# Attention scores as four masked full-array products, the product with v as eight of 66 columns, q scaled before the scores

## The reference

```python
q = rms_norm(layernorm(x) @ w_q.T + b_q, g_q)
k = rms_norm(ctx @ w_k_img.T + b_k_img, g_k_img)      # ctx: 64 rows
v = ctx @ w_v_img.T + b_v_img
p = softmax(q_h @ k_h.T / 4)                          # per head, 64 x 64
x = x + concat(p @ v_h) @ w_o.T + b_o
```

## Time and profile before

| | us |
|---|---|
| median of three runs (911.7 to 912.24) | 911.82 |
| span of the profiled execution | 1005.5 |
| busy in that span: PE / DVE / ACT / POOL | 846.2 / 590.8 / 471.5 / 480.1 |
| attention steps, from the first instruction to 450.7 us and their drain to about 525 | 525 |
| expert tiles, 525 to 875 | 350 |
| combine pass, to the end | 130 |

### The profile page before, as it was taken

One profiled execution on the slowest core, in us unless ns is written; L12 is line 12 of the kernel. 1 busy time (PEld: TensorE's weight loads), 2 busy tenths in 40 slices (PEclk: granted clock), 3 DMA queues, 4 the chain that ended last, 5 costly groups with the idle time before them and its releaser, 6 DMA issues. The chain is left out here.

```text
span 1005.5 us, 21598 instructions
## 1 busy us (share of the span) xinstructions
PE 846.2 (84%) x6034; PEld 685.6 (68%) x6035; DVE 590.8 (59%) x2017; ACT 471.5 (47%) x1411; POOL 480.1 (48%) x684
## 2 busy tenths in 40 slices
PE   5888887988988988887518999999999999899995
PEld 3665555655655655554307888888888888898885
DVE  3666665566565655655524555555556555567786
ACT  3676655656665656655303444444444444333331
POOL 1235434335344344344442555555555555557665
PEclk9989988879798888988557999999999999999998
DMA  6344344334244243346473444443434343267785
GB/s 197 100 126 144 100 131 137 97 125 142 89 136 139 84 135 115 114 127 207 147 210 116 122 125 125 125 125 121 125 120 125 120 125 120 99 217 252 248 249 185
DMA packets 101889, 142.01 MB, mean 141 GB/s; under 512 B 16171, under 2 KB 83043, under 8 KB 101219
## 3 DMA queue, kind: packets, MB, share of 16 engines
q1 hardware_dynamic: 87395, 101.18, 34.2%
q0 software_dynamic: 14080, 38.89, 10.9%
q10 hardware_dynamic: 384, 1.58, 0.5%
HBM read 86.73 MB, written 58.82 MB: 145 GB/s over the span
## 5 line engine op out<-in xcount | busy, mean ns | idle before, releaser
L1309 POOL DMA_INDIRECT yt_d<-yo,name_i x160 | 158.1, 988 | 29.9 <-issue 24.0
L752 POOL DMA_INDIRECT xs_d<-rgu,sloti x128 | 125.5, 981 | 39.6 <-issue 37.5
L1191 PE MATMUL bank<-down_w,rdt 128*128 x320 | 99.6, 393 | 23.3 <-issue 22.7
L1353 DVE TENSOR_TENSOR h<-bank,gated 128x176 f32<-128x176 f32 x160 | 54.7, 342 | 103.4 <-ACT gated L1273 94.8
L1197 PEld LDWEIGHTS bank<-ht,rd_w 88*128 88x128 f32 x640 | 97.2, 192 | 8.2
L768 POOL TENSOR_TENSOR rstd<-mean,mhalf 128x1 f32<-128x1 f32 x32 | 17.5, 548 | 172.5 <-DVE mean L932 172.5
L1307 POOL TENSOR_TENSOR fence<-ones 128x1 f32<-128x1 f32 x160 | 29.6, 185 | 146.2 <-DVE name_i L1344 144.8
L1197 PE MATMUL bank<-ht,rd_w 88*128 88x128 f32 x640 | 97.9, 275 | 0.0
L1269 ACT ACTIVATE rdt<-bank 128x128 f32<-128x128 f32 x160 | 44.4, 278 | 113.2 <-PE bank L1197 111.7
L1273 ACT ACTIVATE gated<-bank 128x176 f32<-128x176 f32 x160 | 50.8, 318 | 88.5 <-PE bank L1213 83.6
L1343 DVE COPY yo<-bank 128x256 f32<-128x256 f32 x160 | 67.1, 419 | 33.1 <-PE bank L1191 32.6
(11 more groups left out here) (163 smaller groups left out, 2072.0 us busy)
## 6 DMA issues: line engine op xcount, KB each, us to landing
xg<-xs_d SPq DMA_DIRECT2D x160, 128.5 KB
got<-yt_d SPq DMA_DIRECT2D x32, 512.0 KB, 4.3
raw<-in_raw SPq DMA_DIRECT2D x32, 496.0 KB
v<-v SPq DMA_DIRECT2D x128, 34.0 KB
xs_d<-in_spare SPq DMA_DIRECT2D x4, 1028.0 KB
xin<-in_x SPq DMA_DIRECT2D x32, 128.0 KB
ctxt<-in_ctxt SPq DMA_DIRECT2D x32, 128.0 KB
xres<-in_x SPq DMA_DIRECT2D x32, 128.0 KB, 3.9
```

Of the source, the lines that this page charges most:

```text
L752: nc.gpsimd.indirect_dma_start(xs_d, bass.IndirectOffsetOnAxis(sloti[:, b, k:k + 1], 0), rgu[:, b, k, :], None)\
L1191: nc.tensor.matmul(y_ps[b], rdt[:, b, :], weight(down_w, DOWN), start=True, stop=True)\
L1309: nc.gpsimd.indirect_dma_start(yt_d, bass.IndirectOffsetOnAxis(name_i[:, b, :], 0), yo[:, b, :], None)\
```

## The change

The four 64 by 256 quarter products of each sequence become two products that use the whole array: q is copied out twice with a mask that keeps the even or the odd heads (`qm`, 128 columns of weights: 2 masks by 64 queries), and k in four copies masked by pairs of heads. So row 64r+q of the scores holds query q and the heads of parity r. The product with v then takes the whole 128 by 128 block of p as weights, with 66 columns (two sets of 32 features and a column of ones); a query's own 16 of 32 features are picked when the result is normalised, in two halves of the partitions. The scale of q by its RMS moves from the exponential to a POOL multiplication of its own (`qn`), and the feature scales move from the copy of q to `k_norm`, which multiplies by a row vector made at the start by two PE products. The columns of the v weights and the rows of w_o and b_v are reordered at the start, by ACT copies and by eight DMAs.

```diff
-                        for blk in range(PAIRS):                       # p_times_v
...
-                            for n in range(2):
-                                m = nc.tensor.matmul(o_ps[SEQ * n:SEQ * (n + 1), pair, :, :],
-                                                     probt[:, b, blk, SEQ * n:SEQ * (n + 1)],
-                                                     v2[:, b, n, :, pair, :], start=True, stop=True)
+                        for n in range(2):
+                            for g in range(BLKS):
+                                m = nc.tensor.matmul(o_ps[:, n, 2 * g:2 * g + 2, :], probt[:, b, BLKS * n + g, :],
+                                                     v2[:, b, n, :, g, :], start=True, stop=True)
...
-                        pe.wait_ge(qb_done, i + 1)                     # qk_turn
+                        pe.wait_ge(qn_done, i + 1)
                         pe.wait_ge(kn_done, i + 1)
...
-                        for c in range(CH):                            # scores
-                            for n in range(2):
-                                for g in range(GROUPS):
-                                    feats = slice(64 * g, 64 * (g + 1))
-                                    m = nc.tensor.matmul(s_ps[SEQ * n:SEQ * (n + 1), g, c * 256:(c + 1) * 256],
-                                                         qt[feats, b, c, SEQ * n:SEQ * (n + 1)],
-                                                         ktm[feats, b, 2 * c + n, :, :], start=True, stop=True)
+                        for n in range(2):
+                            for c in range(CH):
+                                m = nc.tensor.matmul(s_ps[:, n, c * 256:(c + 1) * 256], qm[:, b, 2 * c + n, :, :],
+                                                     ktm[:, b, 2 * c + n, :, :], start=True, stop=True)
...
+                    def gqk_rows():                                    # PE, step 1
+                        pe.wait_ge(set_up, 2 + CH)
+                        for c in range(CH):
+                            m = nc.tensor.matmul(bank5[:, c * P:(c + 1) * P], ones[:, :], gqk_cols[:, c, :],
+                                                 start=True, stop=True)
+                        m.then_inc(gqk_psum, 1)
...
+                        if at_step(s, 1):                              # ACT
+                            act.wait_ge(ld_wkv, 16 * 2)
+                            for c in range(CH):
+                                for x in range(2):
+                                    m = nc.scalar.activation(wkv[:, c, DIM + x * P:DIM + (x + 1) * P]...
...
-                            for c in range(CH):
-                                nc.scalar.activation(qt[:, b, c, :], qkt_ps[:, c, :], ACT.Copy,
-                                                     scale=gqk[:, c:c + 1])
+                            qv = qkt_ps[:, 0:CH, :].rearrange("p c (n q) -> p (c n) q", n=2)
+                            for r in range(2):
+                                nc.scalar.activation(qm[:, b, :, r, :], qv, ACT.Copy, scale=parity[:, r:r + 1])
...
-                            nc.scalar.activation(pb, pb, ACT.Exp, scale=rqk[:, b, 0:1]).then_inc(prob_done, 1)
+                            nc.scalar.activation(pb, pb, ACT.Exp).then_inc(prob_done, 1)
...
                             nc.gpsimd.tensor_tensor(rqk[:, b, :], ssq[:, b, :], mhalf[:, :], ALU.pow).then_inc(rqk_done, 1)
+                            pool.wait_ge(rqk_done, i + 1)
+                            nc.gpsimd.tensor_tensor(qb[:, b, :], qb[:, b, :], rqk[:, b, 0:1].broadcast_to([P, DIM]),
+                                                    ALU.mult).then_inc(qn_done, 1)
...
-                        nc.vector.tensor_tensor(                       # o_norm
-                            ov, o_ps[:, :, :, 0:HD].rearrange("p g r d -> p (g r) d"),
...
+                        for r in range(2):
+                            rows = slice(SEQ * r, SEQ * (r + 1))
+                            m = nc.vector.tensor_tensor(
+                                on[rows, b, :, :, :], o_ps[rows, :, :, r * HD:(r + 1) * HD],
+                                rsum[rows, b, :, :].unsqueeze(3).broadcast_to([SEQ, 2, 2 * BLKS, HD]), ALU.mult)
...
-                        nc.vector.tensor_scalar(kb[:, b, :], kb[:, b, :], rqk[:, b, 1:2], None, ALU.mult)\
-                            .then_inc(kn_done, 1)
+                        nc.vector.scalar_tensor_tensor(out=kb[:, b, :], in0=kb[:, b, :], scalar=rqk[:, b, 1:2],
+                                                       in1=gqk[:, :], op0=ALU.mult, op1=ALU.mult).then_inc(kn_done, 1)
...
+                            for c in range(CH):                        # SP, step 0, before constants(loads_then, ld_then)
+                                half = slice(SEQ * c, SEQ * (c + 1))
+                                for r in range(2):
+                                    src = a["wo"][:, c, :].rearrange("(g r d) n -> r g d n", r=2, d=HD)[r]
+                                    sp.dma_start(wo[half, r, :], src).then_inc(ld_wo, 16)
+                                    src = a["bv"][:, c:c + 1].rearrange("(g r d) n -> r g d n", r=2, d=HD)[r]
+                                    sp.dma_start(bv[half, r:r + 1], src, allow_slow_non_contiguous=True).then_inc(ld_wo, 16)
```

More of the change, by code:

```diff
@@ L130, in build @@
         bv = sb("bv", [P, CH])
+        headmask = sb("headmask", [P, GH])
         gq = sb("gq", [P, CH])
         gk = sb("gk", [P, CH])
-        gqk = sb("gqk", [P, CH])
+        gqk_c = sb("gqk_c", [P, CH])
+        gqk = sb("gqk", [P, DIM])
         rgu_w = sb("rgu_w", [P, CH, DIM + EXPERTS])
@@ L146, in build @@
         bank03 = ps("bank03", [P, 4, 512])
-        bank4, bank5, bank6, bank7 = (ps(f"bank{k}", [P, 512]) for k in range(4, 8))
+        bank45 = ps("bank45", [P, 2, 512])
+        bank4, bank5 = bank45[:, 0, :], bank45[:, 1, :]
+        bank6, bank7 = (ps(f"bank{k}", [P, 512]) for k in range(6, 8))
         loads_first = [(ident, "ident"), (wq, "wq"), (bq, "bq")]
-        loads_next = [(wkv, "wkv"), (bk, "bk"), (gq, "gq"), (gk, "gk"), (headmask, "headmask"), (ones, "ones"),
-                      (bv, "bv")]
-        loads_then = [(wo, "wo"), (bo, "bo"), (rgu_w, "rgu"), (eiota, "eiota"), (tri, "tri"),
+        loads_next = [(bk, "bk"), (gq, "gq"), (gk, "gk"), (headmask, "headmask"), (ones, "ones")]
+        loads_then = [(bo, "bo"), (rgu_w, "rgu"), (eiota, "eiota"), (tri, "tri"),
                       (ebase, "ebase"), (names, "names"), (rd_w, "rd")]
@@ L262, in build @@
             halves_done = asem("halves_done")
+            ld_wkv, wv_done, ld_wo, masks_done, gqk_psum, gqk_done = (
+                asem(n) for n in ("ld_wkv", "wv_done", "ld_wo", "masks_done", "gqk_psum", "gqk_done"))
             sh_psum = asem("sh_psum")
@@ L351, in body @@
                         if at_step(s, 0):
+                            sp.dma_start(wkv[:, :, 0:DIM], a["wkv"][:, :, 0:DIM]).then_inc(ld_wkv, 16)
+                            sp.dma_start(wv_in[:], a["wkv"][:, :, DIM:2 * DIM]).then_inc(ld_wkv, 16)
                             constants(loads_next, ld_next)
@@ L368, in body @@
                             for n in range(2):
[L369 to L371 removed]
+                                for x in range(2):
+                                    sp.dma_start(v2[SEQ * x:SEQ * (x + 1), b, n, x, :, :],
+                                                 v33[SEQ * n:SEQ * (n + 1), b, x, :, :]).then_inc(v2_in[b], 16)
                         i, b = s - 4, ph % 2
@@ L545, in o_turn @@
                         pe.wait_ge(on_done, i + 1)
-                        for c in range(CH):
-                            m = nc.tensor.transpose(pt_ps[:, c, :], on[:, b, c * P:(c + 1) * P], ident[:, :])
+                        for n in range(2):
+                            m = nc.tensor.transpose(pt_ps[:, n, :], on[:, b, n, :, :].rearrange("p g d -> p (g d)"),
+                                                    ident[:, :])
                         m.then_inc(ot_psum, 1)
@@ L648, in body @@
                             nc.scalar.activation(xn1t[:, b, :, :], xnt_ps, ACT.Copy).then_inc(xnt_done, 1)
+                        if at_step(s, 1):
+                            act.wait_ge(ld_wkv, 16 * 2)
+                            for c in range(CH):
+                                for x in range(2):
+                                    m = nc.scalar.activation(
+                                        wkv[:, c, DIM + x * P:DIM + (x + 1) * P].rearrange(
+                                            "p (g r d) -> p g r d", g=BLKS, r=2),
+                                        wv_in[:, c, :].rearrange("p (r g x d) -> p x g r d", r=2, g=BLKS, x=2)[:, x],
+                                        ACT.Copy)
+                            m.then_inc(wv_done, 1)
                         e = s - 1
@@ L778, in _ @@
                     nc.vector.memset(mhalf[:, :], -0.5).then_inc(preset, 1)
```

(23 more changed lines are left out.)

82 lines of the change are left out of this document (43 added, 39 removed).

## The result

| | before | after |
|---|---|---|
| median of four runs, us | 912.03 (911.7 to 918.28) | 942.23 (940.33 to 944.42) |
| ratio, 95% interval | | 1.0295 (1.0258 to 1.0333) |
| profiled execution: own time / span, us | not given / 1005.5 | 944.42 / 942.7 |

The account below looks back on a forecast made before the run. Prediction took the POOL and DVE loop, 12.03 us a step, to bound timed attention steps. Start 1.3, early steps 4.2 and later steps 3.6 gave 9.1 us on 911.8: 921 us, forecast range 914 to 932, 8 in 10 range 890 to 941.

Parts of the forecast that it names:

- What bounds the kernel: Full attention's later steps: timed runs hardly have the trace's two waits, so a step is near 12.0 us, not 15.03.
- late releases: Later attention steps: readers of the scores and the product with v start 1.83 and 2.25 us late while POOL scatters.
- the ring of POOL and DVE: Later attention steps: POOL and DVE hand each other a loop, forecast at 12.03 us a step, above TensorE's 10.31.
- Scores and product with v: TensorE's attention products: scores 1.73 us, +0.71; product with v up to 1.73 us, +0.70 taken with the first load.
- the upper bound: Product with v: 0.108 us per instruction, as a transpose, so 1.73 us; the lower end was 0.9 us.
- `k_norm`, +0.14 us on the loop: DVE in each later step: 0.35 us becomes 0.483 with two SBUF operands, adding 0.14 us.
- The rival for this case: Later steps: `qn` gets ahead of `k_norm`, which waits 0.73 us; 12.90 us a step, 940 us in all; chance 0.11.
- 26 later steps x 0.14: Full attention's later steps: the longer `k_norm` costs 0.14 us in each of 26, together 3.6 us.
- TensorE's limit: Later attention steps: the loop over TensorE, with `o_turn` waiting for `o_norm`, comes to 12.07 us, still under 12.17.
- `qn` at nothing: POOL's 0.73 us `qn` after `rqk`: delays nothing on the loop; `qk_turn`'s wait put at nothing, at most 0.5 us.
- Start, 1.3 us: Kernel start: seven more DMA issues of 0.36 us before the second x tile; up to 2.5 us or nothing, 1.3 taken.
- Early steps, 3 x 1.41: Three attention steps before any scatter, bound by TensorE: each grows from 10.31 to 11.72 us, together 4.2 us.

## Why the prediction was wrong, by its own steps

- **What bounds the kernel**: right. The late releases were of the profiled execution alone, and the ring of POOL and DVE sets the timed step: 11.86 us, 12.03 forecast, because `k_norm` to `sloti` is 4.52 and not 4.70.
- **Scores and product with v**: right, 253.85 - 252.12 = 1.73 us and 255.58 - 253.85 = 1.73; the upper bound taken for the second was the right end.
- **`k_norm`, +0.14 us on the loop**: the step that failed. It is +0.59, 0.94 for 0.35, because `qn` meets it. The rival for this case was in the list at 0.11, with the wrong form: `k_norm` does not wait 0.73 behind `qn`, it starts first and runs 0.46 longer. Against that rival stood that whichever comes first is not delayed; the rows show otherwise. The test that the prediction named (0.8 us or more) came out for it. That its 940 lies near 942 is luck: it had 22.6 us for the later steps and 5.5 for the start and the early steps, and 16.3 and 13.7 were measured.
- **26 later steps x 0.14**: 16.3 us, not 3.6, and `k_norm` is not all of it. TensorE's limit, forecast at 12.07, measured 12.13 and so was about right; but it was set against a ring of 12.03. Against one of 11.86, with the first three of the 26 steps shorter still (10.76 to 11.59), it costs 8.7 us by itself, as the run without `qn` shows. The lengthened ring adds the other 7.6.
- **`qn` at nothing**: right for its own wait, wrong for its neighbour.
- **Start, 1.3 us**: mis-sized, 4.7 between the two profiles. Eight loads took some 0.6 us of SP's queue each (8.22 to 13.01), for seven at 0.36; and the gains' set-up doesn't lie beside the wait for x, since DVE takes it behind that wait.
- **Early steps, 3 x 1.41**: mis-sized, 9.0 us over four steps (73.1 - 59.47 less the start's 4.7). Two steady ones cost about 1.85 each: the 1.38 of the products, 0.22 of wait for the two `o_norm` halves (0.86 us for 0.42), the rest short waits. The two before them cost 2.4 and 2.9, with granted clocks of 0.79 and 0.89 where the kernel before, profiled again, had 1.00. The second of them, 12.83 us at 0.89, took 11.74 and 11.75 at 1.00 in the runs without `qn` and with one load each, so 1.1 of the 9.0 go with the clock of that execution.
- **Sum**: 4.7 + 9.0 + 16.3 = 30.0 for 9.1. The span was forecast at 937 and came at 942.7, which is luck: without the late releases the kernel before has 910.5, not 1005.5 - 78 = 927.5, and the change added 32.2 to it, not 9.

The Trainium skill, SBUF — State Buffer, "Who interferes with whom", states that a DVE instruction with two SBUF inputs and a GpSimd one that reads SBUF exclude each other, the first to start holding the ports. This trace agrees that they interfere (0.94 us for 0.48). It does not agree with who pays: by the records `k_norm` starts 0.04 us before `qn` and is the one that is lengthened, by 0.46 us, less than the 0.61 of `qn`.

## What to carry to other kernels

Where two engines hand a ring to each other, sum that ring from instruction durations and set it beside the busiest engine's row of work: a change costs by what it does to the longer of them, and parts that load different limits don't add up. When two operations like these are released by one semaphore on VectorE and GpSimd, price the one on the ring as if they met. Whether a busy engine (96% here) sets the step is best found by taking work away from it, and the ring's price by moving an instruction inside it: the order on POOL was worth more than the whole change.

## What was not expected of the hardware

- The meeting lengthens VectorE's side by 0.46 us with two operands (0.94 for 0.48, `qn` unchanged at 0.61) and by 0.36 with one (0.71 for 0.35; there `qn` had started 0.18 us earlier and took 0.73).
- One execution of the kernel before held its sub-array products' readers back by about 4 us a step; none of the eight later profiles of kernels with the same products shows it. Its granted clock in that stage was 0.87, and 1.00 in the next profile of the same kernel; which of the two came first is not shown, and why it happened stays open.
- The idle time that POOL shows as issue before a scatter was 0.51 us behind an addition of 0.19 and 0.17 behind one of 0.73.
